# Latent attention phase: loop unrolled, attended heads feed the first output layer, one float32 matmul for the attended sum over values

## The reference, cut to what matters

```
s[h, l] = q[h] . k[g, l]                    # q = (x Wq + bq) of head h, k and v of the group's latents
a[h]    = softmax over l of s[h]            # 100 weights
z[h]    = sum over l of a[h, l] * v[g, l]   # 128 values per head; z has 128 x 128 = 16384 values
n       = |z|                               # one norm over all 16384 values
h1      = silu( (z / n * sqrt(16384) * g1) @ W1 + b1 )      # W1: 16384 x 256
out     = x + silu( (h1 / |h1| * sqrt(256) * g2) @ W2 + b2 )
```

## Time and profile before

| | |
|---|---|
| median of 3 runs | 3522.86 us (3520.49 to 3529.72) |
| profiled execution, its own time | 3516.9 us |
| its span, first to last instruction | 3514.9 us |
| busy share of the span: PE, PEld, DVE, ACT, POOL | 91%, 77%, 69%, 48%, 43% |
| granted TensorE clock, mean | 0.959 |
| the two sequences of `latent` with their closings | from 1557 us to the end |

### The profile page before, as it was taken

One profiled execution on the slowest core, in us unless ns is written; L12 is line 12 of the kernel. 1 busy time (PEld: TensorE's weight loads), 2 busy tenths in 40 slices (PEclk: granted clock), 3 DMA queues, 4 the chain that ended last, 5 costly groups with the idle time before them and its releaser, 6 DMA issues.

```text
span 3514.9 us, 58244 instructions
## 1 busy us (share of the span) xinstructions
PE 3193.8 (91%) x19248; PEld 2700.9 (77%) x19248; DVE 2432.3 (69%) x4411; ACT 1703.7 (48%) x2906; POOL 1507.9 (43%) x1399
## 2 busy tenths in 40 slices
PE   1599799777999999879999999999799999999997
PEld 1355455467888888769888988898789999999996
DVE  1467667644766767667777777777577777777774
ACT  0344344333665656425445544554455555555554
POOL 5411111001100000226666666666466666666663
PEclk9899999979999999989999999999899999999997
DMA  1100000000000000100000100000000000000000
GB/s 40 42 0 0 0 1 0 0 25 33 1 0 0 0 0 0 43 28 28 28 22 26 35 21 28 28 28 28 19 28 27 27 27 27 27 27 27 27 33 6
DMA packets 29103, 69.04 MB, mean 20 GB/s; under 512 B 5581, under 2 KB 9813, under 8 KB 28217
## 3 DMA queue, kind: packets, MB, share of 16 engines
q1 hardware_dynamic: 27448, 64.16, 5.3%
q0 software_dynamic: 1536, 3.15, 0.3%
HBM read 66.25 MB, written 1.05 MB: 19 GB/s over the span
## 4 chain that ended last, share of the span: by engine, by line
PE 47%; issue 5%; POOL 3%; DVE 1%; ACT 0%; POOLq 0%; DVEq 0%; ACTq 0%
PE lat_ps_h L1821 19%; PE lat_ps_z L1835 9%; PE lat_ps_s L1747 7%; PE lat_ps_t L1774 6%; PE lat_ps_z L1765 3%; POOL lat_zz L1554 2%; PE lat_ps_z L1757 2%; PE lat_ps_z L1845 1%; POOL latm_wq L1533 0%; POOL latm_wq L1527 0%; PE lat_ps_s L1863 0%; POOL latm_att L1546 0%; POOL latm_vcg L1538 0%; DVE latm_top L1593 0%; DVE latm_tot L1603 0%
## 5 line engine op out<-in xcount | busy, mean ns | idle before, releaser
L1821 PE MATMUL lat_ps_h<-latm_share,latm_attT 100*128 100x256 f32 x6144 | 893.0, 288 | 5.9 <-issue 5.4
L1821 PEld LDWEIGHTS lat_ps_h<-latm_share,latm_attT 100*128 100x128 f32 x6144 | 825.0, 190 | 30.9 <-DVE latm_attT L1610 10.7
L1546 POOL TENSOR_TENSOR latm_att<-latm_sc,latm_tot 128x400 f32<-128x400 f32 x516 | 440.6, 854 | 647.7 <-DVE latm_tot L1605 620.5
L1554 POOL TENSOR_TENSOR lat_zz<-lat_zz,lat_zsq 128x512 f32<-128x512 f32 x514 | 659.2, 1282 | 0.3
L1682 ACT ACTIVATE latm_sc<-latm_sc 128x400 f32<-128x400 f32 x516 | 278.3, 539 | 439.6 <-DVE latm_sc L1596 439.6
L1835 PE MATMUL lat_ps_z<-latm_attT,latm_vg 100*128 100x512 f32 x1536 | 489.9, 427 | 0.0
L1610 DVE TENSOR_TENSOR latm_attT<-lat_ps_t,latm_attT 100x512 fp32r<-100x512 f32 x514 | 349.9, 681 | 74.3 <-ACT latm_attT L1698 74.3
L1603 DVE TENSOR_REDUCE latm_tot<-latm_sc 128x4 f32<-128x400 f32 x516 | 291.3, 564 | 157.0 <-ACT latm_sc L1682 157.0
L1747 PE MATMUL lat_ps_s<-latm_wk,lat_xr 128*128 128x400 f32 x1548 | 371.0, 348 | 12.2 <-issue 12.2
L1698 ACT CAST latm_attT<-lat_ps_t 100x512 fp32r<-100x512 f32 x514 | 300.4, 584 | 163.6 <-PE lat_ps_t L1774 139.2
L1747 PEld LDWEIGHTS lat_ps_s<-latm_wk,lat_xr 128*128 128x128 f32 x1548 | 291.3, 191 | 61.2 <-issue 15.4
(11 more groups left out here) (352 smaller groups left out, 4728.3 us busy)
## 6 DMA issues: line engine op xcount, KB each, us to landing
lat_w_in<-in_w_quads SPq DMA_DIRECT2D x65, 512.0 KB, 3.5
lat_wq_in<-in_wq_quads SPq DMA_DIRECT2D x65, 256.0 KB, 2.7
moe_w<-in_W SPq DMA_DIRECT2D x2, 1024.0 KB
mha_wqk<-in_Wqk SPq DMA_DIRECT2D x1, 1152.0 KB, 5.1
ret_xpos<-in_xpos_q SPq DMA_DIRECT2D x1, 1024.0 KB, 5.5
ret_xpos<-in_xpos_k SPq DMA_DIRECT2D x1, 1024.0 KB, 4.7
latw_wkv<-in_Wkv SPq DMA_DIRECT2D x1, 1024.0 KB
out<-latm_res SPq DMA_DIRECT2D x2, 512.0 KB, 3.9
```

The source lines that it names most:

```text
L1546: nc.gpsimd.tensor_tensor(att[:, u].rearrange("p (j l) -> p j l", j=QH), sc[:, u].rearrange("p (j l) -> p j l", j=QH), tot[:, u].unsqueeze ...
L1554: nc.gpsimd.tensor_tensor(zz[:, t], zz[:, t], zsq[:, u], ALU.add).then_inc(s["zz_added"], 1)
L1821: mm = e.matmul(ps_h[:, t, :], attT[:, t % 2, a_part, j * P:(j + 1) * P], share[:, u, w_part, j * FF2:(j + 1) * FF2], start=False, stop=Fa ...
```

## The change

- The loop over groups is gone: all 512 steps of both sequences are written out as one stream n = 0..511, followed by 10 steps of closing. The second sequence's steps follow the first's without a break; the closing of the first sequence is spread over the first 72 steps of the second, tile by tile (`closing` gives the step of each stage).
- `share` and its making go. PE makes z of a step with **one float32 matmul** (`reduce_heads`, two instructions in the trace) from `vc` and the unsplit `attT`, into `ps_z`. From `ps_z`, ACT copies the high part (`high_z`), DVE subtracts it for the low part (`low_z`), and ACT squares it (`square`); then the bank is free. The 12 products per step are now z's parts times the parts of g1*W1 (`w1p`, made by POOL `scale_w1`, ACT `high_w1`, DVE `low_w1`, twice per quad).
- The turned weights are copied once, by DVE (`keep_turned`), in place of ACT's high part and DVE's low part.
- The maximum stays on DVE, negated; the subtraction goes into ACT's exponential as a bias, which makes it 4 instructions of 100 columns that read PSUM.
- Square roots and silu of the closing go: DVE computes inverse roots by three Newton steps (15 small instructions for 4 tiles), and silu is made with tanh on ACT and a product on DVE.
- The early part no longer makes `vcT`, nor the split of `vc`.

```diff
-        vcT = m.sb("vcT", [P, B * G + 1, L])
-        vc = m.sb("vc", [L, 2, B * G, D], F32R)
+        vc = m.sb("vc", [L, B * G, D])
         xr = m.sb("xr", [P, 2, NT * P], F32R)
...
-            share = m2.sb("share", [L, 2, 2, QH * FF2], F32R)
+            w1p = m2.sb("w1p", [P, 2, 2, QH * FF2], F32R)
...
-            attT = m2.sb("attT", [L, 2, 2, BANK], F32R)
+            attT = m2.sb("attT", [L, 2, BANK])
+            zr = m2.sb("zr", [P, 2, 2, BANK], F32R)
...
+            def adds_until(n):
+                b, k = n // NS, n % NS
+                return b * (NS - TB) + max(0, k - TB + 1)
+            def closing(i):
+                e = last_of(i)
+                full = last_of(i // GROUP * GROUP + GROUP - 1)
+                pair = i % GROUP // 2
+                if i < TB:
+                    base = NS + TB + TB * i
+                    return {"norm": e + 3 + (i == 0), "affine": full + 4, "tanh": full + 4, "gate": full + 6, "square": full + 6, "power": full + 7,
+                            "turn": base + 5, "result": base + 7, "out_tanh": base + 7, "out": base + 8}
+                return {"norm": e + 3, "affine": full + 3, "tanh": full + 3, "gate": full + 4, "square": full + 4, "power": full + 5,
+                        "turn": full + 6 + pair, "result": full + 7 + pair, "out_tanh": full + 7 + pair, "out": full + 8 + pair}
...
+                def scale_w1(q, half):
+                    e.wait_ge(w1_loaded[q % 2], 16 * (q // 2 + 1))
+                    e.wait_ge(s["w1_ready"], START + max(0, 2 * q + half - 1))
+                    nc.gpsimd.tensor_tensor(w1s[:, half].rearrange("p (j f) -> p j f", j=2), w1_in[:, q % 2, 2 * half:2 * half + 2],
+                                            g1[:, q % NQ, 2 * half:2 * half + 2].unsqueeze(2).to_broadcast([P, 2, FF2]),
+                                            ALU.mult).then_inc(s["w1_scaled"], 1)
...
+                for n in range(K + 1):
+                    q, t = quad(n), n % TB
+                    if n >= 1 and (n - 1) % NS >= TB:
+                        add_squares(n - 1)
+                    if n + 2 < K:
+                        weight(n + 2)
+                    if q + 1 < B * NQ:
+                        if t == 0:
+                            scale_wq(q + 1)
+                        if t == 2:
+                            centre_wq(q + 1)
+                        if t in (4, 5):
+                            scale_w1(q + 1, t - 4)
...
-                def shift(k, u, b, free):
-                    done = b * (NS + 2) + k
-                    e.wait_ge(s["scores_ready"], START + b * (NS + 2) + k + 1)
-                    src = ps_s[:, u, 0:HL].rearrange("p (j l) -> p j l", j=QH)
-                    e.tensor_reduce(top[:, u], src, AX.X, ALU.max).then_inc(s["topped"], 1)
-                    e.wait_ge(s["topped"], START + done + 1)
-                    e.wait_ge(s["weighted"], START + free)
-                    e.tensor_tensor(sc[:, u].rearrange("p (j l) -> p j l", j=QH), src,
-                                    top[:, u].unsqueeze(2).to_broadcast([P, QH, L]), ALU.subtract).then_inc(s["shifted"], 1)
+                def maxima(n):
+                    e.wait_ge(s["scores_ready"], START + n + 1)
+                    e.tensor_reduce(top[:, n % 2], ps_s[:, n % 2, 0:HL].rearrange("p (j l) -> p j l", j=QH), AX.X, ALU.max,
+                                    negate=True).then_inc(s["topped"], 1)
...
-                def low(dst, src, high, made, high_sem, ready):
-                    e.wait_ge(s[high_sem], START + made)
-                    e.tensor_tensor(dst, src, high.bitcast(F32), ALU.subtract).then_inc(s[ready], 1)
...
+                def keep_turned(n):
+                    e.wait_ge(s["turned"], START + n + 1)
+                    e.wait_ge(s["z_ready"], START + max(0, n - 1))
+                    e.tensor_copy(attT[:, n % 2], ps_t[0:L, :]).then_inc(s["attT_ready"], 1)
+                def low_z(n):
+                    u = n % 2
+                    e.wait_ge(s["z_high"], START + n + 1)
+                    e.tensor_tensor(zr[:, u, 1], ps_z[:], zr[:, u, 0].bitcast(F32), ALU.subtract).then_inc(s["z_low"], 1)
...
+                def inverse_root(which, i, floor, done):
+                    x, y = (a[:, which, i:i + GROUP] for a in (sums, inv))
+                    c.then(e.tensor_scalar(x, x, floor, None, ALU.max))
+                    c.then(e.tensor_scalar(y.bitcast(I32), x.bitcast(I32), 1, None, ALU.logical_shift_right))
+                    c.then(e.tensor_scalar(y.bitcast(I32), y.bitcast(I32), -1.0, float(0x5f3759df), ALU.mult, ALU.add))
+                    for n in range(3):
+                        c.then(e.tensor_tensor(newton[:], y, y, ALU.mult))
+                        c.then(e.tensor_tensor(newton[:], newton[:], x, ALU.mult))
+                        c.then(e.tensor_scalar(newton[:], newton[:], -0.5, 1.5, ALU.mult, ALU.add))
+                        c.then(e.tensor_tensor(y, y, newton[:], ALU.mult))
...
+                for n in range(END):
+                    q, t = quad(n), n % TB
+                    next_quad = q + 1 < B * NQ
+                    if 1 <= n <= K:
+                        low_z(n - 1)
+                    if n + 2 < K:
+                        maxima(n + 2)
+                    if t == 3 and next_quad:
+                        low_wk(q + 1)
+                    for i in due(n, "norm"):
+                        norm(i)
+                    for i in due(n, "result"):
+                        project(i)
+                    if 1 <= n < K:
+                        keep_turned(n)
+                    if n + 2 < K:
+                        total(n + 2)
+                    if next_quad:
+                        if t == 1:
+                            mean_wq(q + 1)
+                        if t in (6, 7):
+                            low_w1(q + 1, t - 6)
+                    for i in due(n, "out"):
+                        finish(i)
+                    for i in due(n, "power"):
+                        if i % GROUP == 0:
+                            e.wait_ge(s["power_ready"], START + i + GROUP)
+                            inverse_root(1, i, 4e-24 / FF2, "power_inverted")
+                    for i in due(n, "gate"):
+                        gate(i)
+                    for i in due(n, "affine"):
+                        if i % GROUP == 0:
+                            e.wait_ge(s["norm_kept"], START + i + GROUP)
+                            inverse_root(0, i, 1e-24 / (G * GH * D), "norm_inverted")
+                        affine(i)
...
+                def exponentials(n):
+                    u = n % 2
+                    e.wait_ge(s["topped"], START + n + 1)
+                    e.wait_ge(s["weighted"], START + max(0, n - 1))
+                    for j in range(QH):
+                        last = e.activation(sc[:, u, j * L:(j + 1) * L], ps_s[:, u, j * L:(j + 1) * L], ACT.Exp, bias=top[:, u, j:j + 1])
+                    last.then_inc(s["exped"], 1)
+                def high_z(n):
+                    e.wait_ge(s["z_ready"], START + n + 1)
+                    e.wait_ge(s["added"], START + max(0, n - 1))
+                    e.copy(zr[:, n % 2, 0], ps_z[:]).then_inc(s["z_high"], 1)
+                def square(n):
+                    if n % NS < TB:
+                        e.wait_ge(s["zz_normed"], START + n // NS * (n % TB + 1))
+                        dst = zz[:, n % TB]
+                    else:
+                        e.wait_ge(s["zz_added"], START + adds_until(max(0, n - 2)))
+                        dst = zsq[:, n % 2]
+                    e.wait_ge(s["z_low"], START + n + 1)
+                    e.activation(dst, ps_z[:], ACT.Square).then_inc(s["squared"], 1)
...
+                def free_z(n):
+                    e.wait_ge(s["squared"], START + n)
+                    e.wait_ge(s["z_low"], START + n)
...
+                def add(n, between):
+                    q, t, u = quad(n), n % TB, n % 2
+                    fresh = n % NS < TB
+                    if t == 0:
+                        e.wait_ge(s["w1_ready"], START + 2 * (q + 1))
+                    if fresh:
+                        e.wait_ge(s["h1_kept"], START + n // NS * (t // 2 * 2 + 2))
+                    e.wait_ge(s["z_high"], START + n + 1)
+                    for z_part, w_part in PARTS:
+                        if z_part == 1:
+                            e.wait_ge(s["z_low"], START + n + 1)
                         for j in range(QH):
-                            mm = e.matmul(ps_z[:, t:t + 1], zz[:, t, j * P:(j + 1) * P], ones[:, 0:1], start=(j == 0), stop=(j == QH - 1))
+                            if (z_part, w_part, j) == (0, 0, 3):
+                                between()
+                            first = fresh and t % 2 == 0 and (z_part, w_part, j) == (0, 0, 0)
+                            last = n % NS >= NS - TB and (z_part, w_part, j) == (1, 0, QH - 1)
```

(32 more changed lines are left out.)

553 lines of the change are left out of this document (235 added, 318 removed).

## The result

The changed kernel takes 3792.51 us (median of 4 runs, 3791.03 to 3796.30), the kernel before 3521.95: 1.076 times as long, interval 1.0745 to 1.078. The prediction was 3730 us, range 3590 to 3815. The profiled execution has a span of 3789.5 us, against 3514.9.

The account below looks back on a forecast made before the run. PE bounded the old kernel; the new bound was to be the chain through ps_z and DVE's order. 3516.9 + 250 (steps) - 85 + 59 + 15 - 20 - 11 = 3725, so 3730 us as median; range 3590 to 3815.

Parts of the forecast that it names:

- Plain step 3.55: Ordinary step of the latent phase: z, high part, low part, maximum and copy in turn take 3.55 us, 0.45 more than before.
- The copy at 0.69: DVE's copy of the turned weights, 512 columns from PSUM: 0.69 us, bounds 0.37 and 0.70.
- The four exponentials at 1.08: ACT's four 100-column exponentials per step: 1.08 us against 0.54 for the one before, hidden in a plain step.
- t=3 at 6.0: Step of each 8-step quad that makes wk in ps_z: products, split, copy and hand-over end at 6.0 us.
- t=6 and 7 at 4.2: Two steps per quad that make W1's parts: low_z 0.65 us late each, so 4.2 us.
- t=1 at 3.9: Step of each quad with the mean of wq on DVE: low_z 0.35 us late, so 3.90 us.
- No fetch stalls in the unrolled stream: Straight code of the latent phase: given no idle time for instruction fetch, as the trace showed none within a loop body.
- The third rival: Latent phase: straight code not fetched in time, or the clock falls; 3775 to 3820 us, chance 10%.
- The closings, 59 + 15: First sequence's closing among the second's steps +59 us (bounds 30 and 80); second's closing begun before its last step +15.
- The tail, 26.8: After the last z: remaining norms, roots, last tiles and store take 26.8 us in place of 46.7, so -20.
- The rival that PE stays the bound: Latent steps: copy of turned weights not late, a step under 3.2 us, 3290 us in all; chance 9%.
- The rival of the cheap copy: DVE's copy takes 0.37 us or less, step 3.18 to 3.25, other costs as forecast: 3600 us; chance 13%.

Follow-up runs that it names:

- the reduction ahead of it: Changed kernel plus one extra unused 128-column reduction per step on DVE, right ahead of the copy of the turned weights: 3821.41 us.
- the same reduction behind the sum: Changed kernel plus one extra unused 128-column reduction per step on DVE, behind the sum and reciprocal: 3791.28 us.

## Why the prediction was right, step by step

- **The bound moves from PE to the chain through ps_z and DVE's order**: right, and shown by moving the copy (ratio 1.076 to 1.048), by the reduction ahead of it, which moved the plain steps and no others but t=3, and by the same reduction behind the sum, which left them alone.
- **Plain step 3.55**: 3.67. Two terms of the sum were too small. z was taken as 1.02 from the earlier trace rows, with 1.06 to ACT's start; it is 1.10, and ACT starts after 1.13. The hand-over from the copy to PE was taken as 0.06; the copy ends at 2204.21 and z starts at 2204.36, 0.15. Together 0.16, of which 0.04 came back in low part, maximum and copy: 0.12 x 4 x 64 = 31 of the 49 us by which the steps were undersized. The length goes with PE's idle time just before: in the version with the copy on ACT, z takes 1.02 in the plain steps, where PE comes to it without a pause, and 1.10 behind a wait of 0.33. The hand-over does not: with the centring first, PE had been idle for 0.74 us and began the products of wk 0.05 us behind ACT's square, while it begins 0.15 us behind DVE's copy and behind GpSimd's centring. What makes this difference was not tested. The step lies 0.12 over the forecast, which had allowed 0.1 either way.
- **The copy at 0.69**, chosen between 0.37 and 0.70: 0.68 here. **The four exponentials at 1.08**: 1.04 to 1.06, mean of one 0.352, in plain steps hidden as said. The 0.27 for one does not follow from the two copies that the prediction names, which give 0.23; it follows from the 0.63 of the earlier trace rows with their slope. The Trainium skill's figures ("ScalarE: Activation LUTs", section "What ACT_TABLE_LOAD costs") would have given 1.17, an estimate that the trace does not bear out.
- **t=3 at 6.0**: 6.29. The chain was named right; what was missing was GpSimd. The prediction gave it no part since it has room on average, but its centring stands behind a weighting that waits for DVE's sum. It ties with the square in this kernel: the products begin 0.15 us behind the centring and 0.16 behind the square, and where the square alone was last, they began 0.05 behind it. So the centring costs about 0.1 of the 0.29 here; the rest is the z and the hand-over above. It binds by itself in the versions with shorter steps, where 6.28 stayed until the centring was put first.
- **t=6 and 7 at 4.2**: 4.15, by the chain that was given; the reduction behind the sum moved them alone.
- **t=1 at 3.9**: 4.00, and the size is right in part by luck. The prediction had the mean of wq at 0.85 us less 0.4 of slack and wrote 0.35 late. Two terms came out otherwise: DVE's slack in a plain step is 0.53, and the small instruction, put at 0.2, took 0.34, held by GpSimd's weighting. Low_z is 0.34 late, about half of it (0.18, what the instruction takes over its 0.16) by this wait, for which the prediction had no term.
- **No fetch stalls in the unrolled stream**: right. In the kernel before, unrolled, both sequences take 908 us, and in the changed kernel no wait of PE's matmuls is without a named cause. The third rival had put such stalls, or a fallen clock, at 3775 to 3820, and the measured 3792.5 lies there and not in the forecast's own 3670 to 3790; but its mechanism is not what happened: the granted clock was 1.00 and 0.98 in the two sequences and 0.93 in the 72 us between them (0.98 and 1.00 in the sequences before), and nearly all undisturbed quads take 33.27. The Trainium skill's rule that straight code is fetched ahead and a taken branch may stall ("Runtime: NRT & Kernel Launch", section "Instruction fetch mechanics") agrees with that and with the 36.4 us of turn-backs in the first sequence, but leaves open why the second had none of this size.
- **The closings, 59 + 15**: 84. Around the first sequence's end it is 74 for a predicted 59, at the second's 10 for 15. The two quads at the turn take 48.4 and 56.5 us, and seven quads with a tile's turning, second layer and output among their steps 37.2 to 38.3 in place of 33.3. Moving the closing among the steps was the part of the change that looked like a gain and is none: -48.2 for the gap that goes, +84.4 for the stretched steps, -12.4 at the end, +24 in sum. The steps had no free time in the chain to hide it.
- **The tail, 26.8**: 34.3. The last norms, roots and layers run in turn as before, with less beside them.
- The errors (steps +49, closings +10, tail +8, early part 0) all but one point the same way and add to 67; the range had room for that, the forecast's own width did not. The profiled execution took 3791.3 us for a predicted 3725; the median stands 1 us over it, not 6.

The rival that PE stays the bound (3290) would have needed a plain step of 3.2; no version with the copy on DVE behind low_z and a float32 z had one. The rival of the cheap copy falls with its 0.68.

## What to carry to other kernels

A cheap instruction that nobody waited for late becomes the bound when it stands, on an in-order engine, behind a wait for the chain that it feeds: list for each bank with one buffer the whole round trip, with the queue order on each engine, and do it apart for each kind of step, since here plain steps, t=1, t=3 and t=6 and 7 had different ones. Work put into idle time costs nothing only if the engine is idle in the chain that binds, and if what is beside it lets it run at its own speed: here a VectorE instruction with both inputs in SBUF was held by whatever GpSimd was doing. Unroll for the turn-backs alone where that is what the profile shows: it gave 1.3% here with nothing else touched.

## What the runs showed of the hardware

- A VectorE subtraction with both inputs in SBUF was held while GpSimd's tensor operation ran: 1418 ns on average beside it, 661 where it stood behind the sum and began ahead of GpSimd's next operation, 691 with GpSimd's operation cut to 8 columns. The other way round, GpSimd's weighting took 1.21 us in place of 0.86 when it began 0.16 us behind such a subtraction. A VectorE instruction of only 4 columns with both inputs in SBUF (L1636) ended 0.02 us behind the GpSimd operation that it began beside in all 64 quads of the changed kernel, and 0.02 to 0.03 behind it with the reduction behind the sum, whether it took 0.16 us or 0.60. The subtractions and copies that read PSUM kept their 0.69 and 0.68 beside the same GpSimd work. The Trainium skill ("SBUF — State Buffer", section "SBUF: two separate sides") has the rule that a VectorE operation with two SBUF inputs and a GpSimd operation that reads SBUF exclude each other; these runs agree.
- A float32 product of 512 columns took 1.02 us behind other work and 1.10 after a wait. Three float32r products in its place took 0.93, one 0.47.
- From the end of the last writer to the start of a waiting matmul it took 0.15 us behind VectorE's copy and behind GpSimd's centring, and 0.05 behind ScalarE's square.
- Straight code of the whole latent phase, each line run once, ran without a wait of the matmuls that the profile leaves unnamed, while the loop's turn-backs cost 36.4 us in the first sequence and nothing to speak of in the second. Why the second is spared stays open.
